# A block's four quarters of expert products: from one step into two

## The reference

```
h  = (1 + eps) * layernorm(x) + segment_sum(relu(layernorm(x)[src] + edge_attr @ W_e + b_e), dst)
x1 = x + silu(bn(silu(bn(h @ W1 + b1)) @ W2 + b2))      # bn: over all nodes
n  = layernorm(x1), in groups of 16 tokens
logits = einsum('bgtd,des->bgtes', n, controller) + tie      # 16 experts e, 4 sets s
perm   = (logits == max over the 16 tokens t)                # one token per group, expert, set
inner  = relu(sum over t of (n @ f1)[t, e, s, 32] * perm)    # [group, e, s, 32]
out    = x1 + sum over e, s of (inner @ f2[e, s]) * perm     # back to the token
```

## Time and profile before

| | |
|---|---|
| median of 3 runs | 2024.03 us (2021.88 to 2025.5) |
| the profiled execution | 2019.68 us, span 2018.0 us |
| mean granted clock of TensorE | 0.970 |
| busy: PE, DVE, ACT, POOL | 92%, 59%, 49%, 18% of the span |
| matmuls of line 1520 (quarters) | 5120, in 40 quarters |

### The profile page before, as it was taken

One profiled execution on the slowest core, in us unless ns is written; L12 is line 12 of the kernel. 1 busy time (PEld: TensorE's weight loads), 2 busy tenths in 40 slices (PEclk: granted clock), 3 DMA queues, 4 the chain that ended last, 5 costly groups with the idle time before them and its releaser, 6 DMA issues. The chain is left out here.

```text
span 2018.0 us, 41277 instructions
## 1 busy us (share of the span) xinstructions
PE 1857.1 (92%) x15896; PEld 1362.2 (68%) x15896; DVE 1190.3 (59%) x2345; ACT 988.5 (49%) x1716; POOL 364.5 (18%) x428
## 2 busy tenths in 40 slices
PE   5486899999999899999999879998998989999998
PEld 3354678888888788888888765565655656665654
DVE  6487566666666444333333366676766767667655
ACT  2254223333333386566556255565655657556543
POOL 4486310000000000000000052222222222222210
PEclk9688899999999999999999999999999999999999
DMA  9977756665556364344333263443434434344322
GB/s 368 306 147 106 200 142 183 180 178 164 162 167 190 123 263 155 122 141 164 122 133 131 92 225 114 127 134 105 151 115 128 127 106 158 113 131 137 107 75 69
DMA packets 162435, 305.68 MB, mean 151 GB/s; under 512 B 15506, under 2 KB 87186, under 8 KB 159091
## 3 DMA queue, kind: packets, MB, share of 16 engines
q1 hardware_dynamic: 153327, 282.66, 43.8%
q0 software_dynamic: 8960, 20.98, 5.3%
HBM read 168.72 MB, written 134.87 MB: 150 GB/s over the span
## 5 line engine op out<-in xcount | busy, mean ns | idle before, releaser
L1488 PE MATMUL bank<-f2s,inner_bd 128*32 128x512 f32 x2528 | 300.5, 601 | 6.9 <-issue 6.3
L1372 ACT ACTIVATE inter_hi<-bank 128x512 fp32r<-128x512 f32 x316 | 188.9, 598 | 201.7 <-PE bank L1488 199.9
L598 ACT ACTIVATE h1o<-bank,b_by_channel 128x500 f32<-128x500 f32 x160 | 108.5, 678 | 324.8 <-PE bank L430 316.3
L1294 DVE TENSOR_TENSOR inter_lo<-bank,inter_hi 128x512 fp32r<-128x512 f32 x316 | 216.1, 689 | 84.8 <-ACT inter_hi L1372 83.2
L428 PE MATMUL bank<-hhi,w_hi 128*128 128x500 f32 x624 | 244.7, 392 | 0.0
L430 PE MATMUL bank<-hhi,w_lo 128*128 128x500 f32 x624 | 243.6, 390 | 0.0
L429 PE MATMUL bank<-hlo,w_hi 128*128 128x500 f32 x624 | 242.6, 389 | 0.0
L428 PE MATMUL bank<-ahi,w_hi 128*128 128x500 f32 x608 | 237.3, 390 | 0.0
L429 PE MATMUL bank<-alo,w_hi 128*128 128x500 f32 x608 | 236.6, 389 | 0.0
L430 PE MATMUL bank<-ahi,w_lo 128*128 128x500 f32 x608 | 236.4, 389 | 0.0
L562 DVE BATCH_NORM_STATS2 stats<-h1o 128x500 f32 (+1 forms) x160 | 103.2, 674 | 155.6 <-ACT h1o L598 155.6
(11 more groups left out here) (149 smaller groups left out, 3356.9 us busy)
## 6 DMA issues: line engine op xcount, KB each, us to landing
h1T<-h1o SPq DMA_DIRECT2D x19, 2000.0 KB, 8.0
h1in<-h1T SPq DMA_DIRECT2D x19, 2000.0 KB, 9.7
aggregate<-at SPq DMA_DIRECT2D x20, 1024.0 KB
x<-in_x SPq DMA_DIRECT2D x79, 256.0 KB, 2.6
x<-x SPq DMA_DIRECT2D x79, 256.0 KB, 3.7
x_back<-x SPq DMA_DIRECT2D x79, 256.0 KB, 2.8
out<-x_back SPq DMA_DIRECT2D x79, 256.0 KB, 2.1
h2in<-h2T SPq DMA_DIRECT2D x39, 512.0 KB, 4.0
```

The lines of the kernel that those rows point to most:

```text
L598: nc.scalar.activation(h1o[b][:, m, :], mb[m % 4][:, 0:CW], ACT.Identity, bias=b1c[:, m:m + 1]).then_inc(evr, 1)
L1294: nc.vector.tensor_tensor(ilo[u % QB][:, :], bI[u % QB][:, :], ihi[u % QB][:, :].bitcast(F32), ALU.subtract).then_inc(ilr, 1)
L1372: nc.scalar.activation(ihi[n % QB][:, :], bI[n % QB][:, :], ACT.Copy).then_inc(ihr, 1)
L1488: last = nc.tensor.matmul(bI[b][32 * i:32 * i + 32, :], ibd[:, e, j, :, :].rearrange("p s g -> p (s g)"), f2s[:, e, :], start=True, stop=True)
```

## The change

A step is a "crossing" when the back tile is the last of its block and a front block follows (step 7 of backs 0 to 8). There the sums stand at the head of the step; the units go in the order 2, 3, 0, 1; quarter 0 of the front block stands ahead of the last unit (which is unit 1), quarter 1 between the turns of g and x, quarter 2 ahead of the final product. Quarter 3 follows in step 0 of the next pass, behind its first unit. Block 0's quarters stay as they were. Quarters 0, 2 and 3 now use `bD[0]`, quarter 1 `bD[1]`. Waits follow the new order: those that went by a unit's running number go by its quarter (`lows`), and the final product of a crossing also waits for quarter 1's relus, as it shares their bank.

```diff
+        bQ = [bD[0], bD[1], bD[0], bD[0]]
+        def crossing(kb, j):
+            return kb is not None and kb < NB - 1 and j == tiles(kb) - 1
+        def quarters(kb, j):
+            return (2, 3, 0, 1) if crossing(kb, j) else (0, 1, 2, 3)
+        def quarter(kb, u):
+            return quarters(kb, u // QB)[u % QB]
+        def lows(kb, j, b):
+            kb, j = (kb, j) if j >= 0 else (kb - 1, tiles(kb - 1) - 1)
+            return unit_of(kb, j * QB + quarters(kb, j).index(b)) + 1
...
+                if crossing(back, m):
+                    if ahead:
+                        yield "sums", m
+                    for p in range(3):
+                        yield "unit", u + p
+                        yield "low", u + p
+                    if next_:
+                        yield "norm", m + 2
+                    yield "inner", (front, 0)
+                    yield "unit", u + 3
+                    yield "low", u + 3
+                    if new:
+                        yield "turn_g", m + 3
+                        yield "stats", m + 3
+                    yield "inner", (front, 1)
+                    if next_:
+                        yield "turn_x", m + 2
+                elif behind and m == 0 and back > 0:
+                    yield "unit", u
+                    yield "low", u
+                    if next_:
+                        yield "norm", m + 2
+                    yield "inner", (back, 3)
+                    yield "unit", u + 1
+                    yield "low", u + 1
+                    if new:
+                        yield "turn_g", m + 3
+                    yield "unit", u + 2
+                    yield "low", u + 2
+                    if new:
+                        yield "stats", m + 3
+                    yield "unit", u + 3
+                    yield "low", u + 3
+                    if ahead:
+                        yield "sums", m
+                    if next_:
+                        yield "turn_x", m + 2
...
+                if crossing(back, m):
+                    yield "inner", (front, 2)
                 if behind:
                     yield "final", m
                     yield "result", m
-            if front is not None:
-                yield "inner", 0
+            if front is not None and back is None:
+                yield "inner", (front, 0)
...
                         if h and kb is not None:
-                            pe.wait_ge(ilr, unit_of(kb, j * QB + 1) + 1)
+                            pe.wait_ge(ilr, lows(kb, j - 1 if crossing(kb, j) else j, 1))
...
                     if b < 2:
-                        pe.wait_ge(yr, (k * TB + j if k is not None else NT) * KH)
+                        done = NT if k is None else min(k * TB + j + 1, k * TB + tiles(k)) if crossing(kb, j) else k * TB + j
+                        pe.wait_ge(yr, done * KH)
...
+                    if crossing(kb, j):
+                        pe.wait_ge(inv, (k * QB + 2) * 2)
+                        pe.wait_ge(ina, (k * QB + 2) * 2)
...
+                    if q == 1 and not static(k, 1):
+                        pe.wait_ge(otr, k * TB - 1)
+                    if q >= 2:
+                        last = 0 if q == 2 else 2
+                        pe.wait_ge(inv, (k * QB + last + 1) * 2)
+                        pe.wait_ge(ina, (k * QB + last + 1) * 2)
```

More of the change, by code:

```diff
@@ L999, in schedule @@
                     yield "keep", m // 2
-                if behind and m == 0:
-                    yield "inner", 1
+                if crossing(back, m):
[35 more added lines that the diff above has]
+                        yield "turn_x", m + 2
+                elif behind and m == 0:
+                    yield "inner", (back, 1)
                     yield "unit", u
@@ L1007, in schedule @@
                         yield "turn_g", m + 3
-                    yield "inner", 2
+                    yield "inner", (back, 2)
                     yield "unit", u + 1
@@ L1012, in schedule @@
                         yield "stats", m + 3
-                    yield "inner", 3
+                    yield "inner", (back, 3)
                     yield "unit", u + 2
@@ L1070, in schedule @@
                     yield "result", m
-            if front is not None:
-                yield "inner", 0
+            if front is not None and back is None:
+                yield "inner", (front, 0)
         def relu(op, q, s, *more):
             return op(ibd[32 * s:32 * s + 32, QE * q:QE * q + QE, :, s, :],
-                      bD[q % 2][32 * s:32 * s + 32, 0:QE * TB * GB].rearrange("p (e j g) -> p e j g", e=QE, g=GB), *more)
+                      bQ[q][32 * s:32 * s + 32, 0:QE * TB * GB].rearrange("p (e j g) -> p e j g", e=QE, g=GB), *more)
         def unit_of(kb, u):
             return kb * UNITS + u
-        def block_of(q, k, kb):
-            return k if q == 0 else kb
         with nc.Block() as block:
@@ L1289, in inter_low @@
                 def inter_low(kb, u):
-                    q = unit_of(kb, u)
+                    q, b = unit_of(kb, u), quarter(kb, u)
                     dve.wait_ge(ihr, q + 1)
                     if not static(q, QB):
-                        dve.wait_ge(fp, q - QB + 1)
-                    nc.vector.tensor_tensor(ilo[u % QB][:, :], bI[u % QB][:, :], ihi[u % QB][:, :].bitcast(F32),
+                        dve.wait_ge(fp, (q // QB - 1) * QB + b + 1)
+                    nc.vector.tensor_tensor(ilo[b][:, :], bI[b][:, :], ihi[b][:, :].bitcast(F32),
                                             ALU.subtract).then_inc(ilr, 1)
@@ L1328, in body @@
                         if what == "inner":
-                            dve.wait_ge(inp, block_of(n, k, kb) * QB + n + 1)
-                            if static(block_of(n, k, kb), 1) and n == 0:
+                            dve.wait_ge(inp, n[0] * QB + n[1] + 1)
+                            if static(n[0], 1) and n[1] == 0:
                                 dve.wait_ge(ibz, PIECES)
                             for s in range(0, NS, 2):
-                                relu(nc.vector.tensor_scalar_max, n, s, 0.0).then_inc(inv, 1)
+                                relu(nc.vector.tensor_scalar_max, n[1], s, 0.0).then_inc(inv, 1)
                 blocks(dve, body)
@@ L1367, in body @@
                         if what == "unit":
-                            q = unit_of(kb, n)
+                            q, b = unit_of(kb, n), quarter(kb, n)
                             act.wait_ge(ip, q + 1)
                             if not static(q, QB):
-                                act.wait_ge(fp, q - QB + 1)
-                            nc.scalar.activation(ihi[n % QB][:, :], bI[n % QB][:, :], ACT.Copy).then_inc(ihr, 1)
+                                act.wait_ge(fp, (q // QB - 1) * QB + b + 1)
+                            nc.scalar.activation(ihi[b][:, :], bI[b][:, :], ACT.Copy).then_inc(ihr, 1)
                         if what == "turn_x":
@@ L1380, in body @@
                         if what == "inner":
-                            act.wait_ge(inp, block_of(n, k, kb) * QB + n + 1)
-                            if static(block_of(n, k, kb), 1) and n == 0:
+                            act.wait_ge(inp, n[0] * QB + n[1] + 1)
+                            if static(n[0], 1) and n[1] == 0:
                                 act.wait_ge(ibz, PIECES)
                             for s in range(1, NS, 2):
-                                relu(nc.scalar.activation, n, s, ACT.Relu).then_inc(ina, 1)
+                                relu(nc.scalar.activation, n[1], s, ACT.Relu).then_inc(ina, 1)
                 blocks(act, body)
@@ L1473, in inter @@
                 def inter(k, kb, u):
-                    j, b, q = u // QB, u % QB, unit_of(kb, u)
+                    j, b, q = u // QB, quarter(kb, u), unit_of(kb, u)
                     if b < 2:
-                        pe.wait_ge(yr, (k * TB + j if k is not None else NT) * KH)
+                        done = NT if k is None else min(k * TB + j + 1, k * TB + tiles(k)) if crossing(kb, j) else k * TB + j
+                        pe.wait_ge(yr, done * KH)
                     if static(kb, 1) and u == 0:
@@ L1484, in inter @@
                     if not static(q, QB):
-                        pe.wait_ge(ilr, q - QB + 1)
+                        pe.wait_ge(ilr, lows(kb, j - 1, b))
                     for i in range(NS):
@@ L1497, in final @@
                     pe.wait_ge(yr, min((k * TB + j) * KH + 2, NT * KH) if k is not None else NT * KH)
+                    if crossing(kb, j):
+                        pe.wait_ge(inv, (k * QB + 2) * 2)
+                        pe.wait_ge(ina, (k * QB + 2) * 2)
                     for b in range(QB):
[L1499 removed]
+                        pe.wait_ge(ilr, lows(kb, j, b))
                         nc.tensor.matmul(bF[:, :], rbd[:, b, :], ihi[b][:, :], start=(b == 0), stop=False)
@@ L1520, in inner @@
                                 last = nc.tensor.matmul(
```

(4 more changed lines are left out.)

## The result

The changed kernel took 1993.79 us (median of 4 runs, 1990.82 to 1996.32) against 2023.73 us (4 runs) for the kernel before: ratio 0.9852, 95% interval 0.9833 to 0.987, so 30 us or 1.5% faster. Forecast were 2003 us in a range of 1988 to 2019. Timed again beside other kernels, it gave the same ratio, 0.9857 (0.9838 to 0.9876).

What follows compares the result with a forecast made beforehand. PE bounds the kernel, losing 6.0 us per crossing to code loading. Eight crossings gain 18.5 us, the ninth 2.3, in all 21; profiled 2019.68 falls to 1998.7, plus 4.35 for the runs' median: 2003 us, range 1988 to 2019.

Steps and rivals of the forecast that it cites:

- Code loading as the cause: PE's idle stops in mid-quarter are waits for the next block of about 256 instructions, 3.9 us restart to restart.
- 6.0 us lost per crossing: Steps opening a block: 22.3 us measured against 16.3 us of work and a short wait; the rest lost to stops.
- Sums at the head: Crossing step's start: sums wait for the previous tile's last addition on VectorE, 0.45 us; yT copies just hidden.
- Logits behind X: Crossing step: logits directly after the turn of xn wait for its copy on ScalarE, 1.1 us (0.8 to 1.3).
- Relus and banks: Quarters and final product waiting for earlier quarters' relus in shared banks: no cost, enough other PE work between.
- Code stops after: Code-loading stops left per changed crossing: 2.2 us (0.7 to 5.1), 3.3 in the ninth; gain 21 us in all.
- the first gap: Unit and turn of g between quarters 0 and 1: its code block takes 3.2 us, 0.7 short of 3.9.
- the start: Code block holding quarter 0's beginning: short by 0 to 2.0 us depending on its boundary, taken as 1.0.
- The half clock: After a 3.6 us stop one crossing lost 1.7 us to halved clock; expected none after, with no 3 us stop.
- Rival A: Code stops vanish whole because the gaps cover every round: 41 us gained, 1983 us; chance 0.08.
- Rival B: Code rounds stay long, 5.8 us, beside transfers: 6 us slower, 2030 us; chance 0.05.
- Rival C: Each stop belongs to a quarter wherever it stands, new waits come on top: 14 us slower, 2038 us; chance 0.04.

Runs made afterwards that it cites:

- the reordering alone: Changed kernel's crossing step with all four quarters back in the old kernel's places; 2035.16 us, ratio 1.0093 to the kernel before.
- side-by-side kernel: Changed kernel with quarters 0, 1 and 2 next to each other just ahead of the final product; 2016.21 us, ratio 0.9992 to the kernel before.
- second profile: Profile of the changed kernel, code unmodified, timed again beside other kernels; 1988.88 us, ratio 0.9857 to the kernel before.
- late-load kernel: Kernel before with SyncE's 512 KB load of h2in issued after step 0's output store; 2007.86 us, ratio 0.9952.
- shifted: Kernel before with 24 more warm-up matmuls, 96 more instructions, in the first pass; 2019.01 us against 2018.81.
- light kernels: Kernel before and changed kernel, each with three of four channel chunks left out of the expert products; 1936.99 us (0.9596) and 1931.51 us (0.9569).

## Why the prediction was right, and where its size was off

- *Code loading as the cause* stands: stops always at the same instruction of 256, in other matmuls when 96 instructions are added ahead, gone when the quarters are light, back when they are side by side.
- *6.0 us lost per crossing*: the loss is there, and the reordering alone left it there, but not all of it is code loading. Some 0.4 us is the last unit's wait for quarter 3's relus, which I had not seen, and in three crossings 1.7 us is the half clock.
- *Sums at the head*, 0.45 us: measured 0.48, eight times (3.9 us). The yT copies are hidden by units 2 and 3, as worked out.
- *Logits behind X*, 1.1 us: measured 0.90, and half of this term was wrong in kind. I had put the wait into the gap as cover (4.3 us) and also charged it in full; taking it away gained nothing.
- *Relus and banks*, nothing: right for the kernel after (0.3 us, once). For the kernel before the 0.4 us above was missed; it is a small part of the gain.
- *Code stops after*, 2.2 us per crossing and 3.3 in the last, 21 us: this is the term that was mis-sized. With 8 x 25.5 + 20.0 = 224 us of work and 8 x 1.4 = 11 of new waits, 251.8 leaves 17 us in the first profile and 246.1 leaves 11 in the second; the idle time named issue is 7.5 in the first, so more than half of its 17 us is not named. I had read the round as 3.9 from two restarts of one crossing; the ten rounds of the side-by-side kernel lie at 3.6, from 3.34 to 3.88. With 3.6 the first gap's block (3.2 us) is short by 0.4 instead of 0.7 and the start by at most 1.7 instead of 2.0. That is not the whole difference: four of the eight full crossings have no issue stop of 0.25 us at all in the second profile, so the 1.0 for the start and the 0.5 for transfers were too high for most. No run parts the two.
- *The half clock*: three crossings had it before (0.95 over the pair), one after (0.94), none in the late-load kernel or the changed kernel's second profile. Expected was none, since no stop of 3 us was; the eighth pair of the first profile, 30.78 us, has it all the same, after idle stretches of 1.0 and 0.9 us:

```profile
1860.84 0.54 PE L1577 MATMUL bank<-yT,f1s 128*32 128x64 f32 x22 [1.00 <-issue]
...
1862.88 1.98 PE L1476 MATMUL bank<-xn_T,controller_s 128*64 128x128 f32 x16 [0.92 <-ACT xn_T L1431]
```

  So the premise that it takes a stop of 3 us was wrong; the logits behind the second stretch take 1.9 us instead of 1.0, and the granted clock is 0.65 over 1862 to 1865 us. And a clock of 0.93 over 23.93 us is some 3.4 us at half the clock, which cost 1.7 us; the prediction's words have the two mixed up.
- Rival A (all stops gone, 41 us) was 11 us off, the forecast's 21 us 9: the truth, 30, lies between. The forecast was right in the mechanism and in the new waits. That its 21 us of stops came nearer than A's none owes something to luck: 7.5 us are named as stops, and the other 9 of the first profile's 17 are time that I had not forecast. Rival B needs rounds of 5.6 us; in the first profile of the changed kernel the longest that ended in a stop took 4.5. Rival C is refuted by the side-by-side, the shifted and the light kernels. The rule of the Trainium skill, "Runtime: NRT & Kernel Launch", section "Instruction fetch mechanics", that a border of 256 instructions is mostly hidden, holds in these traces for the ordinary steps and not where 256 instructions execute in 1.92 us.

## What to carry to other kernels

Where PE idles on "issue" in the middle of a run of small matmuls, count the instructions between the stops: an equal count, whatever the code says there, points to code loading, and a packet of the queue of kind "instruction" shortly before each restart (2.2 to 3.2 us here) confirms it. What helps is time per instruction, so put long-running matmuls between the short ones, and let a wait that can't be avoided fall into a stretch that would be short of a round without it; taking the 0.9 us before the logits away gained nothing here. Keep bulk transfers away from it.

## What the hardware showed that was not expected

- A quarter of code, 128 small matmuls with their loads, executes in 1.92 us, and the next block takes 3.34 to 3.62 us from restart to restart with no other DMA packet beside it (side-by-side kernel), 5.26 with a 512 KB load in flight (kernel before) and 3.89 with that load moved.
- The cost of a crossing depends on where the border of a code block falls: adding 96 instructions elsewhere made one step 2.4 us longer (22.41 to 24.80) and others shorter, 6.6 us less over the nine steps.
- The same program's crossings summed to 251.8 us in one profiled execution and 246.1 in another.
